# Self-attention's queries and keys projected turned, for two tiles at a time, and laid out by DMA through DRAM

## The reference

```python
x = x + attn(_layernorm(x))     # q, k, v = x @ Wq.T, ...; 16 heads of 16; each position attends to the
                                # last 64 (itself among them); 63 learned keys and values stand before
                                # the first position; softmax(q.k / 4) @ v; @ Wo.T
x = x + xattn(_layernorm(x))    # 16 heads of 64 over a context of 77 positions, 192 wide
x = x + ffn(_layernorm(x))      # a shared GELU network (256-1024-256) plus 8 expert networks,
                                # of which a router picks 2 for each position
```

## Time and profile before

| | us |
|---|---|
| median of 3 runs | 800.63 |
| lowest, highest | 799.0, 801.41 |
| the profiled execution's own time | 794.88 |
| its span | 793.1 |
| TensorE busy | 732.9 (92%) |
| VectorE, ScalarE, GpSimd busy | 505.1, 487.2, 388.6 |

### The profile page before, as it was taken

How to read it: one execution, slowest core, us unless ns; L and a number is a source line. 1 busy time by engine, 2 the same in 40 slices (tenths; PEclk the granted TensorE clock), 3 DMA queues, 4 the chain that set the end, 5 groups by cost and what they waited for, 6 DMA issues and landing times.

```text
span 793.1 us, 18305 instructions
## 1 busy us (share of the span) xinstructions
PE 732.9 (92%) x5562; PEld 661.1 (83%) x5593; DVE 505.1 (64%) x1185; ACT 487.2 (61%) x1635; POOL 388.6 (49%) x398
## 2 busy tenths in 40 slices
PE   3988999999997499999998889999999999999998
PEld 3977888888885388899898779989998999989997
DVE  5566877878875267899996545555555455543554
ACT  2536888888886287877774345555555555553453
POOL 4012655655644255677775693898437300004630
PEclk9999999999998599999999899999999999999999
DMA  8506122123131000000032142455515211112430
GB/s 213 152 1 213 61 100 106 57 104 107 53 108 68 7 1 1 28 27 26 27 134 86 68 176 96 161 191 179 179 41 179 74 40 40 41 40 67 134 101 28
DMA packets 47628, 69.65 MB, mean 88 GB/s; under 512 B 4989, under 2 KB 39317, under 8 KB 47573
## 3 DMA queue, kind: packets, MB, share of 16 engines
q1 hardware_dynamic: 37253, 39.58, 15.3%
q0 software_dynamic: 8576, 29.10, 11.0%
q10 hardware_dynamic: 1744, 0.28, 0.2%
HBM read 40.76 MB, written 28.18 MB: 87 GB/s over the span
## 4 chain that ended last, share of the span: by engine, by line
PE 59%; DVE 13%; ACT 9%; issue 6%; POOL 3%; DMA 2%; DVEq 0%; ACTq 0%; SPq 0%; POOLq 0%
PE PQ L266 12%; PE PQ L268 11%; PE PQ L267 11%; PE PQ L821 4%; PE PQ L1064 3%; PE PQ L778 3%; ACT prob L1178 3%; PE PQ L806 3%; PE PQ L840 2%; PE PQ L1000 2%; PE PQ L1002 2%; PE PQ L1001 2%; ACT prob L1253 2%; DVE negm L1592 2%; DVE ptl L1354 2%
## 5 line engine op out<-in xcount | busy, mean ns | idle before, releaser
L266 PE MATMUL PQ<-wts,hth 128*128 128x256 f32 x424 | 124.1, 293 | 4.2 <-DVE htl L1354 4.1
L268 PE MATMUL PQ<-wts,htl 128*128 128x256 f32 x424 | 119.4, 282 | 0.0
L267 PE MATMUL PQ<-wts,hth 128*128 128x256 f32 x424 | 119.2, 281 | 0.0
L1178 ACT ACTIVATE prob<-PQ,negm 128x128 f32<-128x128 f32 x256 | 90.5, 373 | 20.1 <-DVE negm L1464 18.4
L1253 ACT ACTIVATE prob<-PQ,negm 128x77 f32<-128x77 f32 x256 | 79.7, 367 | 34.4 <-DVE negm L1592 34.4
L1354 DVE TENSOR_TENSOR htl<-PQ,hth 128x512 fp32r<-128x512 f32 x106 | 69.1, 687 | 47.6 <-ACT hth L1107 47.4
L1107 ACT ACTIVATE hth<-PQ 128x512 fp32r<-128x512 f32 x106 | 58.6, 598 | 48.7 <-PE PQ L1064 48.5
L1324 ACT ACT_TABLE_LOAD x37 | 47.5, 1283 | 62.4 <-DVE PQ L1753 62.4
L266 PEld LDWEIGHTS PQ<-wts,hth 128*128 128x128 f32 x424 | 80.4, 190 | 6.3 <-DVE htl L1354 4.4
L267 PEld LDWEIGHTS PQ<-wts,hth 128*128 128x128 f32 x424 | 80.7, 190 | 0.0
L268 PEld LDWEIGHTS PQ<-wts,htl 128*128 128x128 f32 x424 | 80.4, 190 | 0.0
(11 more groups left out here) (237 smaller groups left out, 2260.5 us busy)
## 6 DMA issues: line engine op xcount, KB each, us to landing
slots<-zeros SPq DMA_DIRECT2D x16, 1024.0 KB, 4.3
raw<-in_L_ffn_exp_w_dram POOLq DMA_DIRECT2D x16, 1024.0 KB, 5.8
xf_sb<-slots SPq DMA_DIRECT2D x39, 128.0 KB, 2.1
slots<-y_sb SPq DMA_DIRECT2D x37, 128.0 KB, 1.7
b_all<-in_L_ffn_exp_b_dram POOLq DMA_DIRECT2D x6, 512.0 KB, 4.2
raw<-in_L_ffn_shared_w_dram SPq DMA_DIRECT2D x2, 1024.0 KB, 6.8
out_dram<-X SPq DMA_DIRECT2D x16, 128.0 KB
X<-in_x_dram SPq DMA_DIRECT2D x1, 1792.0 KB, 23.6
```

The source lines that it names most:

```text
L266: pe.matmul(o, lh, rh, start=start, stop=False)
L267: pe.matmul(o, lh, rl, start=False, stop=False)
L268: return pe.matmul(o, ll, rh, start=False, stop=stop)
L1178: last = nc.scalar.activation(prob[s][:, j, :], self_s[:, s % 2, j * P:(j + 1) * P], ACT.Exp, bias=negm[:, q, u:u + 1], accum_out=den[:, q ...
```

## The change

- q and k of two tiles (a pair, 256 positions) are projected turned: the weights are the stationary side and x of both tiles the moving one, 12 products of 256 columns for k and 12 for q (`keys`, `queries`), so that channels lie on partitions and no transposes of q and k are needed. v stays as it was, a tile at a time (`values`). `qs`, `ks`, the 16 transposes and the copies to Q and K are gone.
- ScalarE and VectorE write the high and low parts of a pair's k and q to `flat` (512 columns each). SP stores each to the DRAM tensor `turned` (`rows_out`, 512 KB in rows of 1 KB) and loads from it into Q and K: 12 DMAs of 32 KB for a tile's queries, in runs of 256 bytes (`queries_in`), and 3 of 128 KB for its keys, in runs of 512 bytes (`keys_in`). The three parts take 96 partitions where they took 128.
- `scores` of a tile's first step waits for these DMAs.
- The loops over tiles are written out on all engines, the order of a tile's products is new (output of step n-3 and transposes of step n-2 behind the scores of step n), the products for a pair's keys and queries stand in the even tile before it, and self_o and self_m alternate between two PSUM banks.
- The clearing of `slots` is issued behind self-attention, and only the first scatter waits for it.

The core of the diff, SP first, then TensorE, ScalarE and VectorE:

```diff
+    PR = 2 * DH
+    SPAN = 2 * P
...
+    turned = nc.dram_tensor("turned", [2, NT // 2, 2, PAIRS, PR, SPAN], F32, kind="Internal").ap()
...
-    kinit = reg.place("kinit", [P, PAIRS, W], F32R)
+    kinit = reg.place("kinit", [3 * PR, PAIRS, W], F32R)
...
-    qs = reg.place("qs", [P, H, 64], F32)
-    ks = reg.place("ks", [P, H, 64], F32)
-    xn = reg.place("xn", [P, D], F32)
-    xth = [reg.place(f"xth{i}", [P, DC, P], F32R) for i in range(2)]
-    xtl = [reg.place(f"xtl{i}", [P, DC, P], F32R) for i in range(2)]
+    r3s = reg.at
+    flat = [reg.place(f"flat_{n}", [P, 2, DC, SPAN], F32R) for n in "qk"]
+    xn = [reg.place(f"xn{i}", [P, D], F32) for i in range(2)]
+    xth = reg.place("xth", [P, DC, SPAN], F32R)
+    xtl = reg.place("xtl", [P, DC, SPAN], F32R)
...
+        def rows_out(which, s, done, p):
+            sp.wait_ge(s, C + p + 1)
+            sp.dma_start(turned[which, p].rearrange("s (g j) r n -> (j r) s g n", g=DC),
+                         flat[which][:, :, :, :].bitcast(F32)).then_inc(done, 16)
+        def queries_in(t):
+            p, u = t // 2, t % 2
+            sp.wait_ge(q_out, 16 * (p + 1))
+            if t < 2:
+                sp.wait_ge(made, 2)
+                sp.wait_ge(v_made, 1)
+            else:
+                sp.wait_ge(a["S"], C + 4 * (t - 1))
+            for c, part in enumerate((0, 0, 1)):
+                for e in range(2):
+                    rows = slice(c * PR + e * DH, c * PR + (e + 1) * DH)
+                    for second in range(2):
+                        at = u * P + second * HB
+                        sp.dma_start(Q[u][rows, :, second, e, :].bitcast(F32),
+                                     turned[0, p, part, :, e * DH:(e + 1) * DH, at:at + HB].rearrange("h r n -> r h n")).then_inc(q_in[u], 16)
+        def keys_in(t):
+            p, u = t // 2, t % 2
+            sp.wait_ge(k_out, 16 * (p + 1))
+            if t:
+                sp.wait_ge(a["S"], C + 4 * (t - 1) + 2)
+            else:
+                sp.wait_ge(a_k0, 1)
+            for c, part in enumerate((0, 1, 0)):
+                sp.dma_start(K[c * PR:(c + 1) * PR, :, 2 * u:2 * u + 2, :].rearrange("p h b n -> p h (b n)").bitcast(F32),
+                             turned[1, p, part, :, :, u * P:(u + 1) * P].rearrange("h r n -> r h n")).then_inc(k_in[u], 16)
...
+        rows_out(1, a["lk"], k_out, 0)
+        keys_in(0)
+        rows_out(0, a["lq"], q_out, 0)
+        queries_in(0)
+        queries_in(1)
         sp.wait_ge(p_pe, CHUNKS)
         sp.dma_start(raw[:, 0:DC * FF].rearrange("p (c f) -> p c f", c=DC),
                      sw1.rearrange("(c p) f -> p c f", p=P)).then_inc(ld_raw, 16)
         sp.dma_start(raw[:, DC * FF:].rearrange("p (c n) -> p c n", c=KF),
                      sw2.rearrange("(c p) n -> p c n", p=P)).then_inc(ld_raw, 16)
+        keys_in(1)
+        for p in range(1, NT // 2):
+            rows_out(1, a["lk"], k_out, p)
+            rows_out(0, a["lq"], q_out, p)
+            queries_in(2 * p)
+            keys_in(2 * p)
+            queries_in(2 * p + 1)
+            keys_in(2 * p + 1)
...
-        with sp.Fori(0, NT) as t:
-            sp.wait_ge(a["S"], C + t * 4)
-            clear(t * E, E)
-        clear(NT * E, 2)
         sp.wait_ge(a["x1"], C + NT)
         sp.dma_start(shared_b2[:, :], sb2.rearrange("(o n) -> o n", o=1).broadcast_to([P, D])).then_inc(ld["biases"], 16)
+        with sp.Fori(0, NT) as t:
+            clear(t * E, E)
+        clear(NT * E, 2)
...
+                if t == 0:
+                    pool.wait_ge(zeroed, 16 * (NT + 1))
...
+        def inputs_turned(p):
+            pe.wait_ge(a["xn"], C + 2 * p + 2)
+            pe.wait_ge(a["lq"], C + p)
+            for u in range(2):
+                for ch in range(DC):
+                    last = pe.transpose(self_x[:, ch * SPAN + u * P:ch * SPAN + (u + 1) * P], xn[u][:, ch * P:(ch + 1) * P], ident[:, :])
+            last.then_inc(a["xT"], 1)
+        def columns(o, m, begin, end):
+            parts = [(g, ch, left, right) for g in range(DC) for ch in range(DC) for left, right in ((0, 0), (0, 1), (1, 0))]
+            for g, ch, left, right in parts[begin:end]:
+                at = m * D + g * P
+                last = pe.matmul(o[:, g * SPAN:(g + 1) * SPAN], (WTh, WTl)[left][:, ch, at:at + P], (xth, xtl)[right][:, ch, :],
+                                 start=ch == 0 and left == right == 0, stop=ch == 1 and left == 1)
+            return last
+        def keys(p, begin, end):
+            if begin == 0:
+                pe.wait_ge(a["xh"], C + p + 1)
+                pe.wait_ge(a["xl"], C + p + 1)
+                pe.wait_ge(a["v"], C + p)
+            last = columns(self_kv, 1, begin, end)
+            if end == 12:
+                last.then_inc(a["k"], 1)
+        def queries(p, begin, end):
+            last = columns(self_x, 0, begin, end)
+            if end == 12:
+                last.then_inc(a["q"], 1)
...
+        def scores(n):
+            t, s = n // 4, n % 4
+            q, second, g = t % 2, s // 2, s % 2
+            if s == 0:
+                pe.wait_ge(q_in[q], 192 * (t // 2 + 1))
+                pe.wait_ge(k_in[q], 48 * (t // 2 + 1))
+                if t % TB == 0:
+                    pe.wait_ge(a_k0, t // TB + 1)
...
+            pe.wait_ge(a["exp"], C + n - 1)
+            ps = self_s[:, s % 2, :]
+            turn = 1 if second or q else 0
+            pe.matmul(ps, identb[:, :], window[:, turn, :, :, :].rearrange("p j e n -> p (j e n)"), start=True, stop=False)
+            for j in range(4):
+                p = 4 * g + j
+                if second:
+                    blocks = K[:, p, 2 * q:2 * q + 2, :]
+                else:
+                    blocks = K[:, p, 1:3, :] if q else K[:, p, 0:4:3, :]
+                last = pe.matmul(ps[:, j * P:(j + 1) * P], Q[q][:, p, second, :, :].rearrange("p e n -> p (e n)"), blocks,
+                                 start=False, stop=j == 3)
+            last.then_inc(a["S"], 1)
...
+        def self_attention(i):
+            t, p = i - 1, (i + 1) // 2
+            odd = i % 2 == 1
+            begins_pair = p < NT // 2
+            has_values = not odd and i < NT
+            for s in range(4):
+                n = 4 * t + s
+                if 0 <= n < 4 * NT:
+                    scores(n)
+                if 0 <= n - 3 < 4 * NT:
+                    output(n - 3)
+                if 0 <= n - 2 < 4 * NT:
+                    transposed(n - 2)
+                if odd and begins_pair:
+                    if s < 2:
+                        keys(p, (0, 8)[s], (8, 12)[s])
+                    else:
+                        queries(p, (0, 8)[s - 2], (8, 12)[s - 2])
+                if has_values and s == 0:
+                    values(i // 2, 0)
+                if s == 1 and is_tile(t - 2):
+                    projected_out(t - 2)
+                if has_values and s == 2:
+                    values(i // 2, 1)
+                    if i // 2 + 1 < NT // 2:
+                        inputs_turned(i // 2 + 1)
         pe.wait_ge(p_act, CH_VW)
         pe.wait_ge(p_dve, CH_VW)
-        turned(0)
+        inputs_turned(0)
         value_products(0)
-        pe.wait_ge(a_k0, 1)
-        sweep_self_attention(pe, self_attention)
+        keys(0, 0, 12)
+        value_products(1)
+        queries(0, 0, 12)
+        value_products(2)
+        values(0, 0)
+        values(0, 1)
+        value_products(3)
+        inputs_turned(1)
+        value_products(4)
+        value_products(5)
+        sweep_self_attention(self_attention)
...
+        def queries_high(p):
+            act.wait_ge(a["q"], C + p + 1)
+            if p:
+                act.wait_ge(q_out, 16 * p)
+            copy(flat[0][:, 0, :, :], self_x.rearrange("p (g n) -> p g n", g=DC), DH ** -0.5).then_inc(a["hq"], 1)
...
+        def self_attention(i):
+            t, p = i - 1, (i + 1) // 2
+            odd = i % 2 == 1
+            if not odd and i < NT:
+                queries_high(i // 2)
+            if is_tile(t):
+                exponentials(4 * t)
+            if is_tile(t - 1):
+                evicted(4 * t - 1)
+            if is_tile(t):
+                exponentials(4 * t + 1)
+            if odd and p < NT // 2:
+                keys_high(p)
+            if is_tile(t - 1):
+                evens(t - 1)
+            if is_tile(t):
+                exponentials(4 * t + 2)
+            if not odd and i // 2 + 1 < NT // 2:
+                x_high(i // 2 + 1)
+            if is_tile(t):
+                evicted(4 * t + 1)
+                exponentials(4 * t + 3)
...
+        def keys_low(p):
+            dve.wait_ge(a["hk"], C + p + 1)
+            less_high(flat[1][:, 1, :, :], self_kv.rearrange("p (g n) -> p g n", g=DC), flat[1][:, 0, :, :]).then_inc(a["lk"], 1)
+        def queries_low_part(p):
+            dve.wait_ge(a["hq"], C + p + 1)
+            dve.scalar_tensor_tensor(flat[0][:, 1, :, :], self_x.rearrange("p (g n) -> p g n", g=DC), DH ** -0.5,
```

(22 more changed lines are left out.)

615 lines of the change are left out of this document (237 added, 378 removed).

## The result

The changed kernel takes 834.63 us (median of 4 runs, 831.85 to 843.18) against 799.82 us (4 runs, 799.0 to 801.41): a ratio of 1.0433, 95% interval 1.0389 to 1.0478. It is slower, as forecast, but by 35 us and not by 11, and 834.63 lies above the range, which ended at 828. The profiled execution took 834.44 us (span 832.7).

A forecast was written before the change was run, and what follows sets the result against it. It took TensorE's pace to bound self-attention, with tile set-up hidden beside it. Terms -28.3 - 1.3 + 30.1 + 9.1 + 1.5 = +11.1 us gave 806.0 us profiled, 811 forecast against the median; range 776 to 828.

The forecast's parts named there:

- The stop: Self-attention, before tiles 2, 4, ..., 14: TensorE waits 4.3 us each for queries and keys through DRAM, +30.1 us.
- Tile 1's keys: Start of tile 1: its key loads, issued behind two 1 MB weight loads, land late, +1.5 us (0 to 3).
- Transposes: Self-attention: the q and k transposes leave TensorE's path, 16 tiles x 1.77 us, -28.3 us.
- the low clock: Self-attention, behind each of seven stops: TensorE runs at the lower clock, 1.3 us each, +9.1 us (0 to 18).
- Start: Before the first probability transposes: products of the next pair fill TensorE's 2.60 us of idle time, -1.3 us.
- clearing: Slot clearing behind self-attention: 54 us, just covered before the first scatter 57.6 us after the stage, 0 us.
- The stages behind: From self-attention's end to the last routed addition: no change in time was forecast, 0 us.
- rival 2: Self-attention: SP becomes the bound, each stop reaches 7.4 us, 834 us in all; chance 0.09.

The follow-up runs named there:

- e4_stale: Changed kernel with queries loaded from the pair before, without waiting for the pair's own store (result not the layer's): 783.5 us, 0.9769 of the kernel before.
- b1_clear_late: Kernel before with only the clearing of the slots moved behind self-attention's last addition: 791.84 us, 0.9994 of the kernel before.
- b3_spare_dmas: Kernel before with 15 spare DMAs more per self-attention tile on SP's queue (twelve of 32 KB, three of 128 KB): 802.54 us, 1.0135 of the kernel before.

## Why the prediction was wrong, step by step

- *The stop, 4.3 us x 7 = +30.1. This step failed, by its size.* The seven were 5.5 to 7.7 us, 45.7 together: +15.6 against the forecast. The mechanism is as told: split, store, twelve and three issues in a row, one landing. The mean is inside the step's own bounds (3.0 to 7.4), but the two longest, 7.47 and 7.71, are beyond them. Over all seven, the issues take 7.1 us instead of 15 x 0.42 = 6.3 (0.43 us each with 0.04 between; +5.5 together); the store takes 23.2 us instead of 7 x 2.8 (+3.6, nearly all of it in the two slow stores above); the scores start 2.1 us behind the last issue instead of 1.7 (+2.9); the odd tile was shorter than 9.7 us (9.0 to 9.2 in five of the seven), which leaves more to wait (+2.8); and the split came at +3.1 us as forecast (3.2), except behind tile 1's stop, where it came at +4.3 (+0.7). I had taken an issue time between two rows (0.34 and 0.46 us) for a kind of DMA that neither of them was, and each tenth of a microsecond counts 15 times per pair.
- *Tile 1's keys, +1.5.* Also too small: the stop there was 6.18 us. The keys' loads were issued at 67.78 to 69.92 us behind the two 1 MB loads, as forecast, but tile 1 was ready at 70.8 where the forecast had 74, and waited to 76.97 where it had 75.5.
- *Transposes, -28.3, and the low clock, +9.1.* Both have the right sign, and together they came out lower than forecast: self-attention's +24.9 less the stops' 51.9 leaves -27.0 where the two terms give -19.2 (on chip C 26.2 less 51.4, -25.2). Apart they can only be estimated. By the starts of the window products a pair takes 23.9 us before, 20.6 to 21.7 in the changed kernel beside its stop, and 19.0 to 19.3 in four of the five pairs that e4_stale's trace shows whole (22.8 in the fifth, where the second batch begins). So two tiles became some 4.8 us shorter, where 3.5 was forecast, and what comes behind a stop costs some 2 us, where 1.3 was. The second price has the lower clock and the refilling of the other engines in it; neither was measured alone. Whole stages give a smaller price (-27.0 against the -31.4 of e4_stale without its stop at tile 1), but that kernel loses some time of its own.
- *Start, clearing.* The first maximum came 0.8 us sooner (forecast 1.3), on chip C 5.5 us later, so the start isn't told to better than that. Clearing was covered, as forecast: the first scatter came 59.0 us behind the last addition (347.7 less 288.7), 58.0 before, and GpSimd did not wait for it (0.36 us of idle time before the scatter, 0.34 before the change). (The expectation of b1_clear_late gives these distances as 57.6 and 58.6.) A clearing DMA landed in 9.8 us, not 4.3, and yet cost nothing, since they overlap. The kernel before with the late clearing agrees (0.9994).
- *The stages behind.* Taken at 0. They were +3.6 us (4.4 on chip C). All three traces of the changed kernel have 455.2 to 455.8 us there, but e4_stale and the kernel with queries first, with the same program behind self-attention, have 451.2 to 451.7, as before the change (450.8 to 453.2). So it isn't the price of that program. Not explained; neither the clearing nor the written-out loops alone reach half a per cent.
- *The last stage, +11.9.* No step had it, and none could from the trace of before. It goes with the chip, since the same kernel has 71.5 us there on chip C.

Of the 28.5 us that the profiled sum missed (39.6 against 11.1), 12.5 are in self-attention, 11.9 in the last stage and 3.6 behind self-attention; the start makes the rest. On chip C, without the last stage's part, the kernel is 32.7 us slower (825.41 against 792.68), near what rival 2 came to (834 us, though its terms add up to 833.4, and the result was 834.63). That is luck: its mechanism is not what happened, SP isn't busy all the time but waits for the split and the store, and the 7.4 us that it charged for each stop are 6.5. By the Trainium skill, "DMA: Bandwidth & Descriptors", section "Issuing engines are not separate DMA queues", issuing is usually small beside the transfer. For one load that is so here (0.47 us to issue, 1.9 us to land), for many that one wait needs it is not: fifteen in a row (7.0 us) cost more than the store and the last load together (5.0).

## What to carry to other kernels

When data must go out and come back within one iteration, write the chain down from the moment the data exist, and count the DMAs that one semaphore waits for: their issues are serial, and each that comes behind the store's landing is worth its time in full. Those that don't need the store go ahead of its landing: three key loads moved there took 12.5 us off seven stops. Give the longest round trip the longest cover: the same DMAs, waited for by halves and with the queries projected before the keys, turned 1.0385 into 0.9826. And compare by stages, between traces of one chip: a stage that the change doesn't touch is a control, and when it moves, look at the recording and the chip before the kernel.

## What the runs showed of the hardware

- The same program, old or new, has a last stage of 71.5 to 72.0 us on two chips and 83.6 to 88.3 us on others, with semaphore steps and landings recorded late or not at all there. The kernel before without spare DMAs was traced only where it takes 71.7 and 71.9.
- A three-dimensional DMA of 32 KB, and one of 16 KB, holds SP's queue 0.43 us, and 0.04 us pass to the next. In a loop with computed addresses (b3_spare_dmas) twelve of 32 KB take 9.1 to 9.9 us, 0.8 each.
- A 512 KB store of queries takes 2.8 to 3.3 us from its issue to the first load behind it, and 3.8 to 4.9 us in each of the ten cases, over five traces, in which a 16 KB load of instructions ran beside it.
- 36,864 packets of 256 and 512 B beside self-attention cost its engines nothing (197.5 us against 197.9 and 198.4 on the same chip).
